# SyncE issues the x halves and half stores of a group ahead of its plain blocks, and loads the block addresses with one register load

## The reference

```python
h = relu(layernorm(x))
for l in range(2):
    m = relu(h[src] + edge_attr)                       # per edge
    sums = segment_sum(m, etype * n + dst)             # per type and node
    mean = sums / max(count, 1)
    h = einsum('rnd,rdo->no', mean, weight[l]) + h @ root[l] + bias[l]
    h = batch_norm(h, gamma[l], beta[l])
    if l == 0: h = relu(h)
return x + h
```

## Time and profile before

| | us |
|---|---|
| median of three runs | 2255.83 (2250.97 to 2261.55) |
| the profiled execution's own time | 2256.96 |
| its span, first to last instruction | 2255.2 |
| PE busy | 1840.5 (82%) |
| DVE busy | 1500.4 (67%) |
| POOL busy | 1332.8 (59%) |
| ACT busy | 1215.8 (54%) |

### The profile page before, as it was taken

The page is one execution under the profiler, slowest core; times in us unless marked ns, Lnnn a source line. Parts: engine busy times, 40 slices in busy tenths (PEclk is TensorE's granted clock), DMA queues, the critical chain, the costliest instruction groups (busy, mean ns, idle before and its releaser), DMA issues. The chain is left out here.

```text
span 2255.2 us, 59542 instructions
## 1 busy us (share of the span) xinstructions
PE 1840.5 (82%) x21976; PEld 1511.3 (67%) x21976; DVE 1500.4 (67%) x4496; ACT 1215.8 (54%) x2596; POOL 1332.8 (59%) x1235
## 2 busy tenths in 40 slices
PE   2379898888888888899788888888888888869866
PEld 1167676766766666799766666666667666769755
DVE  8778898787787776488865555555555555538554
ACT  0157788777777776344334444444444444434555
POOL 6747777666676665300177777777778787631000
PEclk8589999999999999899889999999999999989966
DMA  8824465454554554699734333333333334278699
GB/s 323 324 70 126 136 180 162 143 154 139 154 158 140 149 173 149 243 418 418 296 86 114 103 98 109 93 104 106 95 103 97 111 97 107 75 260 321 240 419 402
DMA packets 265827, 405.66 MB, mean 180 GB/s; under 512 B 35521, under 2 KB 177728, under 8 KB 265534
## 3 DMA queue, kind: packets, MB, share of 16 engines
q1 hardware_dynamic: 202232, 231.29, 31.1%
q0 software_dynamic: 41648, 90.52, 14.4%
q10 hardware_dynamic: 21654, 79.99, 8.8%
HBM read 255.41 MB, written 146.26 MB: 178 GB/s over the span
## 5 line engine op out<-in xcount | busy, mean ns | idle before, releaser
L879 POOL DMA_INDIRECT acc<-arena x408 | 471.4, 1155 | 243.8 <-PE ps_t L1749 125.5
L864 POOL DMA_INDIRECT arena<-h_rows,arena x394 | 437.6, 1111 | 300.3 <-DMA h_rows<-chunk_mem 180.6
L1819 PEld LDWEIGHTS ps_o<-arena 128*128 128x128 f32 x3152 | 401.9, 204 | 221.8 <-DVE arena L1263 203.6
L1819 PE MATMUL ps_o<-arena 128*128 128x128 f32 x3152 | 427.6, 292 | 146.4 <-DVE arena L1263 142.5
L864 POOL DMA_INDIRECT arena<-in_x_dram,arena x394 | 406.1, 1031 | 125.5 <-issue 118.9
L1749 PE MATMUL ps_t<-arena 128*128 128x256 f32 x1576 | 465.7, 420 | 10.7 <-DVE arena L1228 7.1
L1749 PEld LDWEIGHTS ps_t<-arena 128*128 128x128 f32 x1576 | 280.4, 198 | 97.8 <-issue 66.2
L1214 DVE TENSOR_TENSOR arena<-arena,bn_b 128x512 f32<-128x512 f32 (+1 forms) x99 | 68.7, 693 | 363.7 <-DMA arena<-h_rows,arena 363.5
L1228 DVE TENSOR_SCALAR arena<-arena 128x256 f32<-128x256 f32 x788 | 274.3, 410 | 41.0 <-PE ps_o L1769 34.5
L1263 DVE TENSOR_TENSOR arena<-arena 128x640 f32<-128x640 f32 (+2 forms) x396 | 286.8, 765 | 12.0 <-PE ps_y L1824 4.6
L1519 ACT ACTIVATE arena<-ps_t 128x512 f32<-128x512 f32 x396 | 234.3, 592 | 82.5 <-PE ps_t L1749 79.9
(11 more groups left out here) (293 smaller groups left out, 2582.0 us busy)
## 6 DMA issues: line engine op xcount, KB each, us to landing
arena<-in_edge_attr_dram SPq DMA_DIRECT2D x190, 256.0 KB
chunk_mem<-acc SPq DMA_DIRECT2D x55, 512.0 KB, 12.5
acc<-arena ACTq DMA_DIRECT2D x28, 896.0 KB, 23.8
arena<-in_x_dram SPq DMA_DIRECT2D x45, 512.0 KB, 9.7
arena<-acc SPq DMA_DIRECT2D x43, 512.0 KB, 11.0
chunk_mem<-hn_rows SPq DMA_DIRECT2D x41, 512.0 KB, 11.7
out_dram<-arena ACTq DMA_DIRECT2D x38, 512.0 KB, 9.2
h_rows<-chunk_mem ACTq DMA_DIRECT2D x25, 512.0 KB, 7.0
```

The source lines that it names most:

```text
L864: pool.indirect_dma_start(out=hb[:, hb_slot(gg), t // NG, :], out_offset=None, in_=(x, h1_tab)[l], in_offset=at(src_t[:, t:t + 1])).then_i ...
L879: pool.indirect_dma_start(out=acc[l], out_offset=at(idx_t[:, t:t + 1]), in_=ob[:, gg % OB, t // NG, :], in_offset=None, **how).then_inc(co ...
L1819: last = te.matmul(ps_sum[:, c], sm[:, gg % SM, b, j, :], yb[:, gg % 2, b, j, :], start=b == 0, stop=b == NH - 1)
```

## The change

SP issues the x half of the iteration and the store of the half of five iterations back before it waits for the blocks' results, where before it did so behind the blocks. The registers of a group's blocks are read with one load of two values, a stride of `NG` apart, where before each had a load of its own. The same function serves both layers.

```diff
             def window_firsts(g):
-                return {t: sp.value_load(first_i[0:1, t:t + 1], min_val=0, max_val=P * (F + WB * P - 1)) for t in in_window(g)}
+                ts = in_window(g)
+                if not ts:
+                    return {}
+                _, values = nc.values_load_multi_w_load_instructions(
+                    first_i[0:1, ts[0]:ts[-1] + 1:NG], engines=(mybir.EngineType.SP,), min_val=0, max_val=P * (F + WB * P - 1))
+                return dict(zip(ts, values))
...
                     if l > 0 or n >= XB:
                         edge_rows(n, l)
-                    if n >= LAG:
-                        window_rows(n - LAG, l, firsts)
 
                     k = early_half(n)
                     if l == 0 and k is not None:
...
                     k = early_half(n - 5)
                     if l == 0 and k is not None:
                         half_out(k)
+                    if n >= LAG:
+                        window_rows(n - LAG, l, firsts)
```

## The result

| | before | changed |
|---|---|---|
| median, us | 2256.36 (2250.97 to 2261.55, 4 runs) | 2196.78 (2192.15 to 2204.23, 4 runs) |
| ratio to before | 1 | 0.9739, 95% interval 0.9700 to 0.9778 |
| profiled execution: own time / span, us | 2256.96 / 2255.2 | 2204.23 / 2202.5 |

The change makes the kernel 59.6 us faster by the medians, 52.7 us by the profiled executions; the profiled execution of the changed kernel is the slowest of its four.

A forecast was written before the change was run, and what follows sets the result against it. It took the x half's load, held behind `ob_ready` in layer 0's edge stage, as the bound. Gains of 63 us (middle stretch) and 2 us (first half) gave 65 us off 2256.96: 2192, median 2191 us, range 2181 to 2206.

The forecast's parts named there:

- The ring through `ob_ready`: Layer 0 edge stage, middle: x half load tied to ACT's eviction sets 8.75 us a group; DVE's 60.0 us waits go.
- The lead: SP in layer 0: x half issued 5.5 us earlier, net 4.7 us at least; one register load less gives 0.6 us.
- The middle stretch: Layer 0 edge stage, 402.8 to 884.2 us: 481.4 us falls to 418 us, a gain of 63 us, bounds 60 and 71.
- POOL 410.2 us: Middle stretch: POOL is the next limit, with a floor of 410.2 us, 7.46 us a group, its mean instruction staying 1.03 us.
- The coupling on top: Middle stretch: DVE's other waits shrink only in part, so 418 us was taken above POOL's floor of 410.2 us.
- The first half: First x half of layer 0, where DVE stands 8.07 us: issued 1.5 us earlier, gain taken as 2 us, at most 3.7.
- 195 to 395 us, node stages, layer 1: The earlier layer 0 stretch, the node stages and layer 1: gain 0; POOL already full in the earlier stretch and layer 1.
- The signs: Trace, mainly middle stretch: L1185 waits under 8 us, `ob` every 7.5 to 7.7 us, POOL over 95%, clock 0.97 or more.
- The sign that gathers take over: DVE in the middle stretch: if gather waits at L1180, 10.0 us before, take over the wait, the prediction is wrong.
- The PE and DVE ring: Rival, chance 0.20: in layer 0's edge stage PE and DVE wait on each other, taking back 30 us; gain 35, 2221 us.
- SP did get ahead: Against the no-change rival, chance 0.08: SP does not get ahead, x-half waits stay, 2256 us.
- The rival of longer POOL instructions: Rival, chance 0.05: busier DVE lengthens POOL's instructions in the middle stretch; 2312 us if all take 1.46, deciding mean 1.27 us.

The follow-up runs named there:

- order alone: The changed kernel with the old register loads, one per block, so only SP's order differs from the kernel before: 2203.64 us, ratio 0.9747.
- the two changed in layer 1 alone: The changed kernel, in layer 1 with the same-node matrix from one-input operations: 2128.06 us; or without the two broadcast operations of the batch normalisation: 2152.84 us.

## Why the prediction was right, and where its sizes were off

*The ring through `ob_ready`.* Right. Moving the x half alone gave all of it, moving the store alone nothing, and one group more of lead in the old order gave the same. DVE's 60.0 us went to 0.

*The lead.* Right: 6.1 us from issue to use in the half shown, no x-half wait in the stretch. The register load saved 0.35 us a group instead of 0.58, since two values take longer to load than one. By itself it gave 7 us (2 to 12), where the prediction had nothing; why is open: it may be the issue of the half in the old order, which came a little sooner.

*The middle stretch, 481.4 to 418 us.* It came out at 429.9 us, so 51.5 us were won of 63. This is the term that was mis-sized, and by one step: "POOL 410.2 us" took its mean instruction as unchanged. It was 1.062 us instead of 1.032, over 307 instructions 9.2 us. The trace says where they came from. Before, 72 of 305 gathers and scatters in the stretch started during one of DVE's two-input operations (L1211 and L1263, now L1216 and L1268) and took 1.23 us in the mean; in the changed kernel 89 of 306 did, and took 1.29 us. All others took 0.97 us in both. POOL's floor in the stretch came out at 429.9 - (8.9 - 5 x 0.3) = 422.5 us; one instruction more than before in it is 1.4 us, and 1.7 us are other gaps. The coupling on top was 7.4 us, where 418 - 410 = 8 were allowed. This agreement is partly luck: in five other kernels with the x half early and layer 0 otherwise the same (order alone, x half alone, one group ahead, and the two changed in layer 1 alone), the 55 groups took 423.0 to 427.9 us in the profiled execution, with a POOL mean of 1.057 to 1.064 us in all. The longer instructions stand in every one of them, the 7.4 us do not. That POOL's mean did not depend on DVE's share was read from one earlier stretch; in the changed kernel that same stretch has 156.12/145 = 1.077 us, at a DVE share of 84% instead of 86%.

*The first half.* The wait fell from 8.07 to 3.50 us, 4.6 us where 2 were taken: the half was issued 1.9 us earlier and landed in 3.3 us instead of 6.7. Up to group 36 only 2.2 us were left of it. POOL's longer instructions there (1.077 us) may have given the rest back, but this is not shown: in those five other kernels group 36 was filled at 395.1 to 398.8 us, where those with the old order had it at 401.0 to 402.8, so the 2.2 us hang on the execution.

*195 to 395 us, node stages, layer 1.* 0 was right: 0.2 us in layer 1.

*The sum.* The median, 2196.78 us, lies 6 us over the forecast of 2191; the profiled execution, 2204.23, lies 12 over the 2192 of the sum, nearly all of it the middle stretch.

*The signs.* The waits L1190, the clock (0.98), POOL's 97% and layer 1 came as written. `ob` was filled every 7.8 us instead of 7.5 to 7.7, POOL waited 8.9 us for PE instead of 15 to 25, and DVE was busy 87% instead of 88 to 90; longer POOL instructions would do all three. The sign that gathers take over came in part, 10.0 to 20.4 us; with those waits gone the kernel was no faster (2202.44 us), so they were not what set the pace.

*The rivals.* The PE and DVE ring did not take over: L1233 waits 1.4 us instead of 16.9. SP did get ahead. The rival of longer POOL instructions was true in kind and small in size: it needed a mean of 1.27 us to lose the gain, and met 1.06. But what lengthens them is not DVE's busy share. With the one-input form DVE was busy 68% of the layer 1 stretch instead of 54%, and POOL's mean fell. The Trainium skill's page "SBUF — State Buffer", section "Who interferes with whom", has DVE instructions with two SBUF inputs contend with GpSimd instructions that read SBUF. The runs agree with it, 1.162 us against 1.026, both for POOL's indirect DMAs; the prediction should have asked which DVE forms would meet POOL's, not how busy DVE would be.

## What to carry to other kernels

A load that depends on nothing, queued behind a wait for a result, is tied to that result: look for such a load where no engine is full and each waits a little. Before sizing the gain take every engine's waits out of the stretch; the engine with the least to give is the next pace, and its own instruction times must be held against what the others will then do. When POOL with indirect DMAs is the pace, look at which DVE operations run beside them: operations with one SBUF input can be worth more DVE time than they cost where DVE has time to spare, as in layer 1, and lose where it has not, as in layer 0.

## What the runs showed of the hardware that was not expected

- DVE's operations with two SBUF inputs lengthen POOL's indirect DMAs: in layer 1 the mean was 1.162 us with them, 1.085 us without the two of the batch normalisation, and 1.026 us with the same-node matrix in one-input form. The one-input form in layer 1 alone took the kernel from 2197 to 2128 us. The delay falls on the DMA instruction that starts when such an operation is running or about to: 41 that started during L1268 took 1.52 us in the mean, up to 3.10 us were seen, and 178 that started beside no DVE operation took 0.94 to 0.99 us.
- A register load of two values took 822 ns in the median against 584 ns of one.
